# Indirect DMAs of the expert tail at three places in two tile slots, with twelve result buffers

## The reference

```python
x = L0_attn_x
mod = (_silu(L0_c) @ L0_wmod).reshape(L0_c.shape[0], 6, 1, -1)
sa, ca, ga, sb, cb, gb = (mod[:, 0], mod[:, 1], mod[:, 2], mod[:, 3], mod[:, 4], mod[:, 5])
...
h = _layernorm(x, axis=-1) * (1 + ca) + sa
x = x + ga * _L0_attn_ref(h, ...)
h = _layernorm(x, axis=-1) * (1 + cb) + sb
x = x + gb * _L0_ffn_ref(h, ...)
```

```python
confidences = jax.nn.sigmoid(jnp.einsum('bsh,eh->bse', x, conf_w) + conf_b)
bids = confidences * wealth
top_bids, selected_experts = jax.lax.top_k(bids, K)
routing_weights = jax.nn.softmax(top_bids, axis=-1)
...
g = jnp.einsum('bsh,ih->bsi', x, gw)
u = jnp.einsum('bsh,ih->bsi', x, uw)
return jnp.einsum('bsi,hi->bsh', jax.nn.silu(g) * u, dw)
```

## Time and profile before

| what | value |
|---|---|
| median of 3 runs | 612.96 us (611.4 to 614.01) |
| the profiled execution | 611.13 us |
| its span, first to last instruction | 609.4 us |
| mean granted clock of TensorE | 0.966 |
| TensorE busy | 552.1 us |
| VectorE busy | 470.1 us |
| ScalarE busy | 404.2 us |
| GpSimd busy | 244.4 us |
| sends (line 2177) | 71, 973 ns each |
| scatters (line 2069) in the whole program | 64 |

### The profile page before, as it was taken

How to read it: one execution, slowest core, us unless ns; L and a number is a source line. 1 busy time by engine, 2 the same in 40 slices (tenths; PEclk the granted TensorE clock), 3 DMA queues, 4 the chain that set the end, 5 groups by cost and what they waited for, 6 DMA issues and landing times.

```text
span 609.4 us, 16545 instructions
## 1 busy us (share of the span) xinstructions
PE 552.1 (91%) x5257; PEld 416.9 (68%) x5258; DVE 470.1 (77%) x1593; ACT 404.2 (66%) x715; POOL 244.4 (40%) x328
## 2 busy tenths in 40 slices
PE   5787999999999999999999989999889999999920
PEld 2464555666566566575666549998779999999920
DVE  5899778889899899898998757875846666667635
ACT  4424788888878888788778876765445656565511
POOL 5401301041453643535535345666553333333326
PEclk9597999999999999999999999999999999999975
DMA  4441576732242332333331011122422211111147
GB/s 124 133 139 53 152 209 178 206 98 81 72 123 83 89 105 81 114 88 94 109 98 55 16 42 42 41 58 65 109 67 54 54 44 51 46 46 51 36 176 250
DMA packets 61511, 56.82 MB, mean 93 GB/s; under 512 B 11156, under 2 KB 55572, under 8 KB 61444
## 3 DMA queue, kind: packets, MB, share of 16 engines
q1 hardware_dynamic: 56548, 44.88, 26.6%
q0 software_dynamic: 4320, 8.99, 4.7%
q10 hardware_dynamic: 576, 2.10, 0.9%
HBM read 36.92 MB, written 18.45 MB: 91 GB/s over the span
## 4 chain that ended last, share of the span: by engine, by line
PE 75%; DVE 7%; issue 5%; DMA 4%; ACT 3%; POOL 2%; SPq 1%; another core or an unknown queue 1%; POOLq 0%; ACTq 0%; DVEq 0%
PE psN L970 16%; PE psO L570 13%; PE psO L981 8%; PE psT L551 8%; PE psN L536 7%; PE psT L553 5%; PE psN L538 5%; PE psM L578 2%; DMA probs<-expert_out 2%; DVE negm L1415 1%; PE psM L596 1%; PE psM L601 1%; PE psM L644 1%; PE psM L606 1%; PE psT L957 1%
## 5 line engine op out<-in xcount | busy, mean ns | idle before, releaser
L1415 DVE TENSOR_REDUCE negm<-psN 128x1 f32<-128x512 f32 (+3 forms) x352 | 210.9, 636 | 31.5 <-PE psN L538 27.2
L1098 ACT ACTIVATE probs<-psT 128x512 f32<-128x512 f32 x320 | 180.4, 595 | 40.4 <-PE psT L553 32.1
L970 PE MATMUL psN<-probs 128*128 128x128 f32 x1136 | 139.5, 275 | 0.7 <-issue 0.4
L970 PEld LDWEIGHTS psN<-probs 128*128 128x128 f32 x1136 | 132.6, 192 | 1.6 <-issue 1.5
L2177 POOL DMA_INDIRECT expert_out<-kst_all,dest x71 | 69.1, 973 | 108.2 <-DVE kst_all L1932 98.5
L536 PE MATMUL psN<-kst_all,qst_all 74*128 74x256 bf16 (+2 forms) x384 | 101.2, 281 | 6.2 <-DVE negm L1415 4.1
L551 PE MATMUL psT<-qst_all,kst_all 74*128 74x256 bf16 (+2 forms) x384 | 99.7, 277 | 1.6 <-DMA qst_all<-mrow 0.6
L570 PE MATMUL psO<-probs,vaug 128*32 128x512 f32 (+3 forms) x1024 | 93.7, 444 | 0.1
L538 PE MATMUL psN<-kst_all,qst_all 117*128 117x128 bf16 x512 | 91.7, 222 | 0.0
L1292 ACT ACTIVATE probs<-gu_w 128x1024 f32 x70 | 74.0, 1057 | 24.8 <-PE psN L970 20.0
L1908 DVE TENSOR_TENSOR probs<-probs,psN 128x512 f32<-128x512 f32 x71 | 48.7, 686 | 53.4 <-PE psN L970 22.7
(11 more groups left out here) (242 smaller groups left out, 739.5 us busy)
## 6 DMA issues: line engine op xcount, KB each, us to landing
qst_all<-q_parts_dram SPq DMA_DIRECT2D x96, 96.0 KB
kst_all<-k_parts_dram SPq DMA_DIRECT2D x96, 96.0 KB
kst_all<-dispatched SPq DMA_DIRECT2D x71, 66.0 KB
q_parts_dram<-qparts SPq DMA_DIRECT2D x24, 128.0 KB
k_parts_dram<-kparts SPq DMA_DIRECT2D x24, 128.0 KB
xall<-in_x SPq DMA_DIRECT2D x8, 256.0 KB, 3.4
gu_w<-in_gateT SPq DMA_DIRECT2D x4, 512.0 KB, 5.1
gu_w<-in_upT SPq DMA_DIRECT2D x4, 512.0 KB, 4.9
```

What stands on the lines that cost most here:

```text
L970: mm = pe.matmul(bank[par][:, c * P:(c + 1) * P], ew[par][:, half, c * P:(c + 1) * P], xgT[par], start=True, stop=True)
L1098: nc.scalar.activation(probs[:, g % 2, 512 * u:512 * (u + 1)], psT[:, u % TBANKS, :], ACT.Exp, scale=SOFTMAX_SCALE).then_inc(exp_done, 1)
L1415: nc.vector.tensor_reduce(dst, src, axis=AX.X, op=ALU.max, negate=True).then_inc(nat_done, 1)
```

## The change

GpSimd's part of the tail is written anew. In every tile j that is odd there is now one place for an indirect DMA, behind a wait for the gate half of tile j (`g_full`). In every even tile there are two: the first behind a wait for the weighing of tile j-1 (`y_ready`), the second behind a wait for the up half of tile j (`u_full`). Three tables say at which places (tile, place) the scatters of batches 5, 6 and 7 go; every other place sends the oldest tile not yet sent, if there is one older than j. So sends fall behind while the scatters go out.

For that the result buffers and destinations are twelve instead of six; `y_at` names the buffer of a tile and how many sends of that buffer came before. `weights` of tile j waits for the send of tile j-12. And nine turns (`HEAD_ALL`, 54 tiles) are written out on all engines ahead of the hardware loop instead of five. Scatters of batch 6 now begin in tile 12 (before: 10), and those of batch 7 end in tile 24 (before: 25). What is computed does not change.

```diff
+HEAD_ALL = HEAD + 4
+N_ALL = U * HEAD_ALL
+Y = 2 * U
...
-        dest = [sb(f"dest{i}", [P, 1], I32) for i in range(U)]
+        dest = [sb(f"dest{i}", [P, 1], I32) for i in range(Y)]
...
-        ysb = [carve(space_k, E) for _ in range(U)]
+        ysb = [carve(space_k, E) for _ in range(Y)]
...
+        IN_TAIL = ((0, 1), (2, 1), (4, 1), (6, 1), (8, 1))
+        NEXT_TAIL = ((12, 0), (13, 0), (14, 0), (14, 1), (15, 0), (16, 0), (17, 0), (18, 0))
+        LAST_TAIL = ((18, 1), (19, 0), (20, 1), (21, 0), (22, 0), (23, 0), (24, 0), (24, 1))
...
+        def y_at(i, u):
+
+            if isinstance(i, int) and i < HEAD_ALL:
+                return (U * i + u) % Y, (U * i + u) // Y
+            return u, i + (len(range(u, N_ALL, Y)) - HEAD_ALL)
...
-            with sp.Fori(HEAD, TURNS - 1) as i:
+            for j in range(N1, N_ALL):
+                tile_in(*divmod(j, U))
+            with sp.Fori(HEAD_ALL, TURNS - 1) as i:
...
-            with pe.Fori(HEAD, TURNS - 1) as i:
+            for i in range(HEAD, HEAD_ALL):
+                turn(i)
+            with pe.Fori(HEAD_ALL, TURNS - 1) as i:
...
-                if not (isinstance(i, int) and i == 0):
-                    dve.wait_ge(y_out[u], 16 * i)
+                r, sent = y_at(i, u)
+                if not (isinstance(i, int) and sent == 0):
+                    dve.wait_ge(y_out[r], 16 * sent)
...
-                V.tensor_scalar(ysb[u], psY, dsc[u][:, 3:4], None, ALU.mult).then_inc(y_ready, 1)
+                V.tensor_scalar(ysb[y_at(i, u)[0]], psY, dsc[u][:, 3:4], None, ALU.mult).then_inc(y_ready, 1)
...
-                if j % 2 == 1 and IN_LAST + j // 2 < 2 * TB:
-                    scatter(L - 2, IN_LAST + j // 2)
-                if 10 <= j < 10 + 2 * TB:
-                    scatter(L - 1, j - 10)
-                if 18 <= j < 18 + 2 * TB:
-                    scatter(L, j - 18)
+
+            def scatter_or_send(j, place, tiles_sent):
+
+                for b, places, first in ((L - 2, IN_TAIL, IN_LAST), (L - 1, NEXT_TAIL, 0), (L, LAST_TAIL, 0)):
+                    if (j, place) in places:
+                        scatter(b, first + places.index((j, place)))
+                        return tiles_sent
+                if tiles_sent < j:
+                    send(*divmod(tiles_sent, U))
+                    return tiles_sent + 1
+                return tiles_sent
...
-            for j in range(N1):
+            tiles_sent = 0
+            for j in range(N_ALL):
                 ahead(j)
-                send(*divmod(j, U))
-            with pool.Fori(HEAD, TURNS - 1) as i:
+                if j % 2 == 1:
+                    pool.wait_ge(g_full, j + 1)
+                    tiles_sent = scatter_or_send(j, 0, tiles_sent)
+                else:
+                    if j > 0:
+                        pool.wait_ge(y_ready, j)
+                        tiles_sent = scatter_or_send(j, 0, tiles_sent)
+                    pool.wait_ge(u_full, j + 1)
+                    tiles_sent = scatter_or_send(j, 1, tiles_sent)
+            send(*divmod(tiles_sent, U))
+            with pool.Fori(HEAD_ALL, TURNS - 1) as i:
```

More of the change, by code:

```diff
@@ L235, in adaln_attention_moe @@
         y_full, dsc_chain, y_ready = sem("y_full"), sem("dsc_chain"), sem("y_ready")
-        y_out = [sem(f"y_out{i}") for i in range(U)]
+        y_out = [sem(f"y_out{i}") for i in range(Y)]
         yp_in = [sem(f"yp_in{i}") for i in range(B)]
@@ L364, in all_steps @@
                 step(s // G, s % G)
+        def y_at(i, u):
+            if isinstance(i, int) and i < HEAD_ALL:
+                return (U * i + u) % Y, (U * i + u) // Y
+            return u, i + (len(range(u, N_ALL, Y)) - HEAD_ALL)
         def pairs_in(eng, first):
-            for u in range(U):
-                eng.wait_ge(y_out[u], 16 * (TURNS if u < LAST else TURNS - 1))
+            for u in range(Y):
+                sent = len(range(u, N_ALL, Y))
+                if u < U:
+                    sent += TURNS - HEAD_ALL - (u >= LAST)
+                eng.wait_ge(y_out[u], 16 * sent)
             for b in range(first, B, 2):
@@ L1319, in _ @@
                 between(j)
-            with act.Fori(HEAD, TURNS - 1) as i:
+            for i in range(HEAD, HEAD_ALL):
+                turn(i)
+            with act.Fori(HEAD_ALL, TURNS - 1) as i:
                 turn(i)
@@ L1925, in weights @@
                 V.tensor_tensor(d[:, 3:4], d[:, 0:1], d[:, 1:2], ALU.add).then_inc(dsc_chain, 1)
-                V.tensor_tensor(dest[u][:], d[:, 2:3], m[:, C_TOK:C_TOK + 1], ALU.add).then_inc(dsc_chain, 1)
+                V.tensor_tensor(dest[r][:], d[:, 2:3], m[:, C_TOK:C_TOK + 1], ALU.add).then_inc(dsc_chain, 1)
             def weigh(i, u):
@@ L1953, in _ @@
                 weights(*divmod(j, U))
-            with dve.Fori(HEAD, TURNS - 1) as i:
+            for i in range(HEAD, HEAD_ALL):
+                turn(i)
+            with dve.Fori(HEAD_ALL, TURNS - 1) as i:
                 turn(i)
@@ L2166, in ahead @@
                     count(L)
-                if j % 2 == 1 and IN_LAST + j // 2 < 2 * TB:
-                    scatter(L - 2, IN_LAST + j // 2)
-                if 10 <= j < 10 + 2 * TB:
-                    scatter(L - 1, j - 10)
-                if 18 <= j < 18 + 2 * TB:
-                    scatter(L, j - 18)
+            def scatter_or_send(j, place, tiles_sent):
[7 more added lines that the diff above has]
+                return tiles_sent
             def send(i, u):
                 hold("pool", pool, y_ready, U * i + u + 1)
-                gp.indirect_dma_start(yd[:, :], bass.IndirectOffsetOnAxis(ap=dest[u][:, 0:1], axis=0),
-                                      ysb[u], None).then_inc(y_out[u], 16)
-            for j in range(N1):
-                ahead(j)
-                send(*divmod(j, U))
-            with pool.Fori(HEAD, TURNS - 1) as i:
+                r, _ = y_at(i, u)
+                gp.indirect_dma_start(yd[:, :], bass.IndirectOffsetOnAxis(ap=dest[r][:, 0:1], axis=0),
+                                      ysb[r], None).then_inc(y_out[r], 16)
+            tiles_sent = 0
+            for j in range(N_ALL):
+                ahead(j)
+                if j % 2 == 1:
[9 more added lines that the diff above has]
+            with pool.Fori(HEAD_ALL, TURNS - 1) as i:
                 for u in range(U):
```

## The result

The changed kernel takes 614.64 us (median of 14 runs, 612.59 to 618.27); the kernel before takes 612.29 us beside it (14 runs, 609.73 to 614.01). The ratio is 1.0044, with a 95% interval of 1.0028 to 1.006 (the ratios here are those on record, not quotients of two medians): slower by 2.35 us, where the sum said 0.8 us less and the forecast was 612.2 us. The range held it, the direction was wrong.

What follows compares the result with a forecast made beforehand. TensorE, busy 552.1 of 609.4 us, was taken as the bound. Terms of -3.8 (tiles 23 to 29), +3.0 (29 to 43), -0.4 and +0.4 summed to -0.8 us: median 612.2 us, range 605.5 to 616.5.

Steps and rivals of the forecast that it cites:

- The bursts: GpSimd's tail DMAs: bursts behind a weighing shrink from four to three, do not break up, and go on to tile 41.
- the bursts of three stall nothing: Rival: a pair's slack swallows the hold, p = 5.58, median about 606.5 us; 0.35 for faster, shared with other cases.
- the places do what their waits say: Rival: bursts break up, DMAs go singly behind gate and up halves, nothing held; counted within the 0.35 for faster.
- The crux: Tiles 23 to 43: everything hangs on p, a pair of tiles' length; change 10p - 60.9 us, zero at p = 6.09.
- the length of a pair: Two tiles with a burst of three, in tiles 23 to 43: taken as 6.01 us, bounds 5.58 and 6.33.
- Way (i): Pair's length from tiles 23 to 29: measured 7.29 us less one DMA of 1.275 us, giving 6.01 us.
- Way (ii): Pair's length summed from weighing to weighing: 6.03 us with a hold of 1.63 us, 6.33 with 1.93.
- The first tiles: Early scatters put four DMAs in a row instead of three: +0.4 us, bounds 0 and +1.3.
- Tiles 13 to 23: Ten tiles whose stalls are about half not GpSimd's: -0.4 us, bounds 0 and -2.3.
- Twelve buffers: Result buffers of the tail: VectorE never waits for a send; needed, but worth 0 us.
- The written-out turns: Tiles 30 to 53 written out instead of looped: no stall to give back, 0 us.
- The slower rival: Tiles 29 to 43 lose more than earlier tiles win: p = 6.33, +3.7 us, median 616.7; slower by over 0.5%, 0.21.

Runs made afterwards that it cites:

- e5: The changed kernel as it stands, rerun on a chip where nothing is held: 601.53 us, 1.0001 of the kernel before.
- e9: The changed kernel unchanged, run once more on another chip where nothing is held: 601.42 us, 0.9997 of the kernel before.
- e2: The changed kernel without GpSimd's waits for g_full and u_full: 602.22 us, 1.0015 of the kernel before, on a chip where nothing is held.
- e17: The changed kernel as it stands, on a chip that holds signals: 611.71 us, 1.0025 of the kernel before.
- e16: The changed kernel with its three places waiting for later TensorE signals from tile 12 on, on a chip that holds: 604.18 us against 611.68, 0.9864.
- e18: The changed kernel with GpSimd's old DMA order, twelve buffers and written-out tiles kept, on a chip that holds: 610.30 us, 0.9986 of the kernel before.
- e7: The changed kernel with the silu of even tiles 18 to 44 also waiting until the burst's third DMA has landed: 624.38 us, 1.0405 of the kernel before.
- e1: The changed kernel with GpSimd's old DMA order, the rest kept, on a chip where nothing is held: 600.64 us, 0.9995 of the kernel before.
- e3: The changed kernel with the odd tile's place waiting for the weighing, so two DMAs, then one: 601.14 us, 1.0004 of the kernel before.
- e4: The changed kernel with GpSimd's waits set one tile later from tile 12 on: 601.51 us, 1.0008 of the kernel before.
- e8: The changed kernel with the old DMA order, silu of even tiles 16 to 26 also waiting for the burst's fourth DMA to land: 618.43 us, 1.0302 of before.
- e10: The changed kernel with the odd tile's place waiting for the weighing, on another chip where nothing is held: 601.65 us, 1.0022 of the kernel before.
- e14: The changed kernel with places waiting for later TensorE signals from tile 12 on, where nothing is held: 602.04 us, 1.0004 of the kernel before.
- e6: The changed kernel with the odd tile's place waiting for the weighing, on a chip where nothing is held: 600.88 us, 0.9995 of the kernel before.

## Why the prediction was right in its mechanism and wrong in its direction

*The bursts* came as worked out: four became three, they did not break up, the waits on `g_full` and `u_full` were over when GpSimd arrived, and the silu of every even tile from 22 to 44 was held. The prediction's "until the burst has about landed" was too late an end for the hold: by the profile a send lands 2.3 us after its issue (median, e5 and e9), and the held silu starts 1.8 us after the last DMA does. The rival "the bursts of three stall nothing" is what chips A, B and C show (A by e2) and was false where the prediction was measured; "the places do what their waits say" was false everywhere.

*The crux was right, its number was not.* Ten pairs change by 10p - 60.9 us. With the measured 18.62 + 43.40 us for ten pairs p is 6.20 (6.13 on chip F, by e17), and the formula gives +1.1 us; the rows give -3.24 + 4.36 = +1.12. **The step that failed is the length of a pair, taken as 6.01 us**, 0.08 below the zero at 6.09, and measured 0.11 above it. Both ways to it were off. Way (i), 7.29 less one DMA, started from a mean of three unequal pairs: the transposes give 7.15, 7.61 and 7.10 us, and only the middle one follows a silu held to the full 4.68 us. In the other two the word for the silu slips out earlier, at 3.97 and 3.25 us, and the one held to the end is the up half's, for VectorE's multiply. In the kernel before, the third of these pairs:

```profile
446.81 0.27 PE L957 MATMUL psT<-identf,kst_all 128*128 128x128 f32 x1
...
454.42 0.27 PE L957 MATMUL psT<-identf,kst_all 128*128 128x128 f32 x1
454.52 1.95 PE L970 MATMUL psN<-probs 128*128 128x128 f32 x16
...
457.29 0.97 POOL L2069 DMA_INDIRECT dispatched<-kst_all,slots_last  x1 [0.31 <-issue]
...
457.77 0.60 ACT L1300 ACTIVATE probs<-psN 128x512 f32<-128x512 f32 x1 [3.04 <-remote]
...
459.33 0.69 DVE L1908 TENSOR_TENSOR probs<-probs,psN 128x512 f32<-128x512 f32 x1 [3.52 <-issue]
```

(446.81 is the transpose of tile 25 and begins the middle pair.) Way (i) also took the spacing of the DMAs, 1.275 us, for what one of them is worth in the hold, which is 1.4 us (below): 7.61 less 1.4 is 6.2. Way (ii) put the hold's end 1.63 us after the last DMA's start, from a burst of two. In these traces the hold's end moves away from the last start as the burst grows: 1.63 us for two (460.20 to 461.83 in e16), 1.82 for three (466.24 to 468.06), 1.93 for four. From chip to chip it differs by some 0.1 us (on F 1.74 for three, 1.81 for four). With 1.82 us way (ii) gives 6.22. I had leant on the mean because it had three measurements behind it; one clean pair would have been the better row.

*Where the bursts end.* The prediction let them go on to tile 41 and closed the sum at 43. By its own count one send is still behind at tile 41, so that the places of tiles 42 and 43 make one more burst, and GpSimd comes to it when TensorE is at tile 44. Their row goes on to tile 45, and tiles 43 to 47 cost +1.19 us that stood nowhere. This and p (1.9 us over ten pairs) make the wrong sign: 1.9 + 1.2 - 0.8 = +2.3, and the other terms' errors, some tenths each, cancel.

*The first tiles* came at +0.81 us, inside the bounds of 0 and +1.3, twice what I took; F has the same (15.38 against 14.62), and B none. The multiply of tile 3 is 1.38 us later than the 376.00 of the earlier trace rows, where 1.3 was worked out:

```profile
375.48 0.96 POOL L2093 DMA_INDIRECT dispatched<-rows,slots  x1 [0.30 <-issue]
...
377.38 0.69 DVE L1929 TENSOR_TENSOR probs<-probs,psN 128x512 f32<-128x512 f32 x1 [3.98 <-issue]
```

The slack took 0.57 us of that, not most of it. The 1.24 us of the earlier trace rows leave out the 0.24 us between a weighing's end and the down projection that waits for it (469.65 and 469.89 in the timeline above); the rest is open. *Tiles 13 to 23* came at -0.66 for -0.4, and on chip F at +0.28 (34.90 in e17, 34.62 in e18).

*What was costed at nothing.* Twelve buffers: no wait of VectorE for a send appears. The written-out turns: tiles 47 to 70 are 0.20 us shorter, which is all that could be given to them. The Trainium skill (Runtime: NRT & Kernel Launch, Instruction fetch mechanics) has a taken branch wait for a fetch when its target is not among the pages at hand. No more than those 0.20 us is seen here.

*The slower rival* named the mechanism and the side that came true, at p = 6.33. By the Trainium skill's price (DMA: Bandwidth & Descriptors, Anatomy of one DMA) p would have been 6.55, an estimate from its 2.15 us. The trace has 6.20. As a price of the landing, 2.15 us is near the profile's median of 2.3 to 2.4 us for a send; where the silu waited for the landing itself, in e7, it came 2.4 to 4.3 us after the start.

*What the prediction could not know* is that the hold depends on the chip. Its range was made for one value of it; the same kernel costs nothing that can be told on chips B and C (e5, e9).

## What to carry to other kernels

When a burst of GpSimd's DMAs makes other engines late, making the bursts shorter but more numerous can lose: multiply the stall per pair by the pairs it now meets, and take the stall from an instance whose chain of waits is read through, not from a mean of pairs that differ. Ask how late the waiter may come (here an estimated 2.66 us) and space the DMAs until the hold fits into that; e16 issued the same DMAs and was 7.5 us faster than before. Before undoing parts, run before itself on the chip at hand: an effect that its time does not show cannot be studied there.

## What the runs showed that I had not expected

- *Chips differ.* Before takes 600.4 to 601.4 us on three chips and 610.6 to 611.7 on three others, and nearly all of the difference is held signals: from tile 2 to 70 the kernel of e1 takes 201.57 us on chip A and, as e18, 210.53 on chip F. What differs in the chips no run tells.
- *The traces differ too.* Where signals are held, many records of semaphores are missing: the trace has the landing of 0 to 8 of the 71 sends, on chips A, B and C of 20 to 63. Whether the recording of a run has a part in the hold, or both come from one cause, was not tried; every timed run here has its span and clock on record, so none shows the time without recording.
- *The hold grows by more than the DMAs' spacing.* From the first DMA's start to the silu it is 2.95 us for two (458.88 to 461.83), 4.37 for three (463.69 to 468.06) and 5.75 for four (445.85 to 451.60): 1.4 us for each DMA, where GpSimd issues one every 1.275. The first of the three is from chip E and the other two from the first measurement; on chip F three take 4.28 us (tile 30 of e17) and four 5.63 (tile 24 of e18), 1.35 more. What takes the 1.4 us was not tried.
- *A single DMA holds nothing* even where bursts do (the silu at 463.75; the earlier trace rows).
- *A dip of the clock.* In the profiles of e2, e3, e4, e7, e8, e10 and e14 tiles 10 to 13 take 14.4 us instead of 12.8. In e2 the granted clock falls to 0.50, the lower of TensorE's two levels (1.2 for 2.4 GHz), with TensorE busy all the time:

```profile
400.00:402.00 2.00, 2.00 (x14) 2.00 (x14) 0.43 (x3) 1.34 (x3) 1.70 (x2) 0.65 0.30 92
402.00:404.00 2.00, 2.00 (x11) 2.00 (x11) 1.64 (x17) 1.71 (x2) 1.09 (x2) 0.50 0.10 33
404.00:406.00 2.00, 2.00 (x20) 2.00 (x20) 1.09 (x4) 1.14 (x2) 0.00 (x0) 1.00 0.30 79
```

  It costs 1.6 us and falls on one profile and not on another of the same kernel (e3 and e10 have it, e6 has not). Seven of the 13 profiles on chips A, B and C have it, and none of the seven where signals are held. Of the 3.0 us by which e10's span exceeds e9's it makes half; the rest lies mostly ahead of tile 2. It is part of the spread between runs, not of any edit.
